# ScalarE's front end steps placed by each sorting stage's share of VectorE's work

## What is computed

```python
corr = jnp.einsum('bmf,bnf->bmn', x3, x3) / F      # x3: layer-normed x, 4 x 4096 x 256
s = -jnp.sort(-corr, axis=-1)
pooled = jnp.take(s, ranks, axis=-1)               # 256 ranks of 4096
...
x = x + pooled
t = layernorm(x)                                   # per token
h = (t @ W_gat); attention over edges -> scores; top 2 of 4 experts, softmax -> g
for ei in range(4):
    hh = gelu(t @ W1[ei] + b1[ei])
    out = out + g[..., ei] * (hh @ W2[ei] + b2[ei])
x = x + out
```

## Time and profile before

| | us |
|---|---|
| median of 3 runs (31820.22 to 31832.84) | 31830.1 |
| the profiled execution | 31848.84 |
| its span in the trace | 31846.8 |
| VectorE busy, share of the span | 28882.6 (91%) |
| TensorE busy | 25804.8 (81%) |
| ScalarE busy | 21288.4 (67%) |
| GpSimd busy | 17887.8 (56%) |

### The profile page before, as it was taken

How to read it: one execution, slowest core, us unless ns; L and a number is a source line. 1 busy time by engine, 2 the same in 40 slices (tenths; PEclk the granted TensorE clock), 3 DMA queues, 4 the chain that set the end, 5 groups by cost and what they waited for, 6 DMA issues and landing times. The chain is left out here.

```text
span 31846.8 us, 518866 instructions
## 1 busy us (share of the span) xinstructions
PE 25804.8 (81%) x174835; PEld 11870.4 (37%) x175348; DVE 28882.6 (91%) x31110; ACT 21288.4 (67%) x31407; POOL 17887.8 (56%) x9076
## 2 busy tenths in 40 slices
PE   3888888888888888888888888888888888863374
PEld 3555533333333333333333333333333333323364
DVE  6888859999999999999999999999999999996744
ACT  1777777777777777777777777777777777750010
POOL 0000018888888888888888888888885000004510
PEclk8999999999999999999999999999999999985655
DMA  2000000000000000000000000000000000001103
GB/s 89 2 2 2 2 18 5 7 6 7 8 7 12 6 7 7 7 7 7 8 12 7 7 6 7 7 7 7 13 7 6 6 6 6 6 5 14 12 11 131
DMA packets 651262, 396.25 MB, mean 12 GB/s; under 512 B 424844, under 2 KB 604048, under 8 KB 646160
## 3 DMA queue, kind: packets, MB, share of 16 engines
q1 hardware_dynamic: 337746, 311.41, 3.1%
q0 software_dynamic: 290304, 22.40, 1.1%
q10 hardware_dynamic: 20288, 25.70, 0.2%
HBM read 196.48 MB, written 162.34 MB: 11 GB/s over the span
## 5 line engine op out<-in xcount | busy, mean ns | idle before, releaser
L1495 POOL DMA_INDIRECT sorted_d<-word_s,place_s x8192 | 16895.5, 2062 | 2644.0 <-issue 2475.4
L1393 ACT ACTIVATE z<-psum 128x1024 f32<-128x1024 f32 x14208 | 14111.6, 1027 | 3637.2 <-PE psum L1154 2513.6
L1154 PE MATMUL psum<-z,net 64*64 64x512 f32 x103424 | 13419.6, 612 | 2473.1 <-ACT z L1393 2318.9
L1352 DVE TENSOR_TENSOR arena<-arena 128x1536 f32<-128x1536 f32 (+17 forms) x6016 | 11646.3, 1936 | 865.1 <-ACT arena L1432 374.8
L1353 DVE TENSOR_TENSOR arena<-arena 128x1536 f32<-128x1536 f32 (+17 forms) x6016 | 11640.5, 1935 | 0.0
L1154 PEld LDWEIGHTS psum<-z,net 64*64 64x64 f32 x103424 | 3103.5, 131 | 11626.9 <-issue 11612.6
L1646 POOL DMA_INDIRECT arena<-table_d,arena x752 | 918.3, 1221 | 5133.2 <-issue 4647.1
L1432 ACT ACTIVATE arena<-arena 128x2048 f32<-128x2048 f32 (+15 forms) x5248 | 3150.1, 600 | 436.3 <-DVE arena L1353 435.9
L979 ACT ACTIVATE arena<-cst,arena 128x128 bf16<-128x128 f32 x8320 | 2633.5, 389 | 606.8 <-PE psum L907 509.8
L1489 POOL DMA_DIRECT2D word_s<-words_d x64 | 37.8, 591 | 4799.3 <-issue 4665.7
L1161 PE MATMUL psum<-z,net 64*128 64x512 f32 x8192 | 1913.4, 600 | 201.5 <-ACT z L1393 190.3
(11 more groups left out here) (218 smaller groups left out, 18950.4 us busy)
## 6 DMA issues: line engine op xcount, KB each, us to landing
sorted_d<-word_s,place_s POOLq DMA_INDIRECT x8192
y_d<-ys SPq DMA_DIRECT2D x256, 256.0 KB, 2.1
arena<-y_d SPq DMA_DIRECT2D x64, 1024.0 KB, 5.6
arena<-in_x SPq DMA_DIRECT2D x34, 512.0 KB, 5.2
x<-in_x SPq DMA_DIRECT2D x65, 256.0 KB, 2.8
xnt_d<-arena SPq DMA_DIRECT2D x32, 512.0 KB, 3.1
hk_d<-arena SPq DMA_DIRECT2D x32, 512.0 KB, 4.3
arena<-hk_d SPq DMA_DIRECT2D x4, 4096.0 KB
```

The source lines that it names most:

```text
L1154: last = nc.tensor.matmul(psum[n * HALF:(n + 1) * HALF, 2 * s + r, :], b.net[rr, at:at + HALF], flat[rr, n * BANK:(n + 1) * BANK], start=T ...
L1352: nc.vector.tensor_tensor(hi_out, hi_in, lo_in, ALU.max)
L1393: last = nc.scalar.activation(flat, bank, ACT.Abs)
L1495: pool.indirect_dma_start(out=b.sorted_d[:, :], out_offset=bass.IndirectOffsetOnAxis(ap=place_s[:, s, j:j + 1], axis=0), in_=word_s[:, s, ...
```

## The change

The ticks are given to halves of stages instead of stages, and not evenly. `half_of` estimates how many elements VectorE handles in a half of stage s, `cost_of` how long a tick takes by its kind, by the FFN pieces behind it and by ScalarE's copies. `spread_ticks` lays the 120 ticks in order over the 96 halves of 48 stages, so that the sums of both run alike; a tick goes behind the carry of the half in which its middle falls. `period` reads the table. The numbers of ticks per half were 1 or 2; now they are 0 to 3. A stage whose half is short (the second of each merge, where the carry is longest) gets fewer ticks, those behind it more.

```diff
--- before.py
+++ after.py
@@ -1064,10 +1064,46 @@
     FRONT_STEPS = N_STAGES - 2
     FRESH_READ = FIRST_MERGE + 1 if LO > 0 else 1
 
-    def ticks_of(step):
-
-        at = [min(PER_PAIR * n // FRONT_STEPS, PER_PAIR) for n in (step, step + 1)]
-        return list(range(*at))
+    ALONE = 150
+    TENSOR = {"corr": 3300, "wires": 2100, "tile": 600, "swapped": 1050, "full": 1050}
+    SCALAR, PIECE, NEWTON = 1080, 1300, 1500
+
+    def half_of(s):
+
+        p, k = STAGES[s]
+        if s >= N_FULL:
+            return sum(2 * op[4] * op[5] * (2 if k > 1 else 1) + ALONE for kind in
+                       (RANK_OPS if k == 1 else SPARSE_OPS[k]) for op in kind) // 2
+        there = M - (LO if s < FIRST_MERGE else 0)
+        later = (3 * P + D if s == ADD_AT else D + NEWTON if s == NORM_AT else 0)
+        return there - (there // p * k if k < p else 0) + 2 * ALONE + later
+
+    def cost_of(tick):
+
+        j, t = TICK_OF[tick]
+        n = SLOTS
+        ats = [tick - EXPERT_TICK - e * EXPERT_TICKS for e in range(EXPERTS)]
+        ups = sum(1 for at in ats if 0 <= at < HC // 2)
+        downs = sum(1 for at in ats if DOWN_AFTER <= at < DOWN_AFTER + 2)
+        return max(n * TENSOR[FRONT[j][t][0]] + 2 * PIECE * (ups + downs), n * SCALAR)
+
+    def spread_ticks():
+
+
+        spans = [half_of(s) for s in range(FRONT_STEPS) for _ in range(2)]
+        costs = [cost_of(tick) for tick in range(PER_PAIR)]
+        scale = sum(spans) / sum(costs)
+        out, at, done, tick = [], 0, 0.0, 0
+        for span in spans:
+            at, here = at + span, []
+            while tick < PER_PAIR and done + scale * costs[tick] / 2 <= at:
+                here.append(tick)
+                done, tick = done + scale * costs[tick], tick + 1
+            out.append(here)
+        out[-1] += range(tick, PER_PAIR)
+        return out + [[] for _ in range(2 * (N_STAGES - FRONT_STEPS))]
+
+    TICKS_BEHIND = spread_ticks()
 
     with nc.Block() as block:
         @block.sync
@@ -1447,12 +1483,10 @@
 
             def period(i, has_next, has_last):
                 for s, (p, k) in enumerate(STAGES):
-                    ticks = ticks_of(s)
                     for g in range(2):
                         if k < p and s < N_FULL:
                             carry(i, s, g)
-                        middle = len(ticks) // 2
-                        for tick in (ticks[middle:] if g else ticks[:middle]):
+                        for tick in TICKS_BEHIND[2 * s + g]:
                             if has_next:
                                 front(i + 1, tick)
                             if has_last:
```

## The result

The changed kernel takes 32187.1 us in the median of four runs (32145.7 to 32218.1), the kernel before beside it 31827.0 (31820.2 to 31832.8). The ratio is **1.0112, 95% interval 1.0099 to 1.0124**. The forecast was +195 us; the measured difference is +360 us. The profiled execution took 32194.5 us, its span is 32192.4. In the rows of after, VectorE's merging stage is L1388 and L1389, its last four stages are L1352, and a product of TensorE is L1190 (L1154 before).

What follows compares the result with a forecast made beforehand. The chain of TensorE's products and ScalarE's copies was taken as the bound, 375.9 us a pair; terms summing to +4.3 made 380.2, +3.15 against 377.05, times 62 pairs +195 us: 32025 us, range 31900 to 32095.

Steps and rivals of the forecast that it cites:

- the front end: Chain of TensorE's products and ScalarE's copies from tick to tick; claimed 375.9 us a pair if never held up.
- Rival 1: Sorting pairs: VectorE is the bound and its waits for carries go, 370.2 us less, so 31460 us; chance 5%.
- (a): Ticks 69 to 75: carries of stages 28 and 29 now stand before ticks 69 to 71; +2.1 us a pair.
- (d): Ticks 25 and 26: the carries of stage 10 move to ticks 24 and 25; -0.8 us a pair.
- (b): Ticks 95 to 102: tick 95 gets GELUs, a 1.91 us carry and copies one after the other; +1.9 us.
- (c): Layer norm's square root and table load move from ahead of tick 20 to plain tick 17; +1.0 us.
- (e): Ticks 1 to 6: carries from before ticks 2 and 3 both stand before tick 1; +0.4 us.
- the base: Front end's length before the change: 377.05 less waits of 0.8 and 0.3, so 375.9 us a pair.
- the low end: All 1.9 us of ScalarE's waits for VectorE delay the front end: length 375.15 us, result 31976 us.
- the high end: The front end's 1.1 us a pair isn't regained: +4.3 x 62 gives 32097 us.

Runs made afterwards that it cites:

- the fillers: Changed kernel with extra TensorE matmuls, whose result nobody reads, ahead of ticks 2, 71 and 96; 31977.5 us, ratio 1.0042.
- the old start: Changed kernel with the even split back in stages 0 to 7; profiled execution, the fastest of four, 32452 us.
- experiment 4: Changed kernel with the even split back in stages 0 to 7, plus two more ticks ahead of the carries of stage 16; 32036.1 us, ratio 1.0056.
- the tight order: Kernel before, with each carry put where TensorE's product is long and not late for VectorE; 31596.7 us, ratio 0.9922.
- The four moves: Kernel before, with carries of stages 9 to 14 later and some of 29, 30, 39, 40 one tick earlier; 31551.1 us (0.9906), second chip 31941.9 (0.9907).
- The half-sort kernels: Kernel before and changed kernel, each with VectorE's minimum left out of the sorting pairs; 39956 and 40331 us, later pairs 374.9 and 382.4 us.

## Why the prediction was right or wrong

**Right: what bounds the kernel.** The step on which the sign rested, that the front end is the nearer chain and that VectorE's waits hide little, held: the front end's own 374.9 us a pair stands above VectorE's 371.1, and with the new order the pair is the front end's length to 0.3 us. Rival 1 (VectorE's gaps as the gain) had no part in it: VectorE's waits before stages 17, 31 and 41 went, and it waits elsewhere, for longer: 2.1 us before stage 19, 2.0 before 29 and 0.9 before 2, as forecast, and 1.3 before stage 10, which I had not named.

**Right: the order's terms.** With the fillers, (a) to (d) came to +1.9, +2.0, +1.0 and -1.1 for +2.1, +1.9, +1.0 and -0.8, and (e) to +0.6 for +0.4. The single ticks named came out too: 70 at 4.57 (4.6), 95 at 5.08 (5.0), 17 at 3.34 (3.2).

**Short in size: the base.** "I take 0.3 as its mean" and 0.8 for the wait at stage 45 gave a hold-up of 1.1 us a pair; with VectorE's minimum left out, the front end is 2.1 shorter. The two waits themselves were sized right (0.84 and 0.27). The other 1.0 us stands at ticks for which the sum had nothing (0, 12, 24, 117, 118), with its cause open. The bound I kept for the low end (375.15 us) came nearer to the length, but for another reason than the one given; its sum is also 3 us off (2.4 x 62 gives 31979, not 31976). The short base makes the result lower, by some 60 us, and hides a part of the other error.

**Wrong, and the one that put the time outside of the range: the durations of TensorE's work were taken as constant.** The sum priced what ScalarE does ahead of a tick and kept all products at the length they had in the trace of before, where the clock is at its upper level almost throughout (1.00 in the earlier trace rows). Two carries, or GELUs and a carry, ahead of one tick make TensorE wait longer at one go than anywhere at those ticks of the kernel before; behind such a wait its clock was often lower, and product and pieces took nearly twice as long, on the chain that sets the pair. That is 382.7 - 379.1 = 3.6 us a pair, 224 us; in the whole run the fillers gave some 225 back, of which up to 73 were already lost in the kernel before. The trace of before did have the sign: 170.7 us at the lower level, with 18 falls in tick 0 alone, behind waits of about 2 us. Neither end of the range held a term for it: the high end, 32095, was the whole order price without any relief, and nothing else. Ticks 71 and 97, which I had put at 3.47 each, are at 4.27 and 4.35; with fillers both are at 3.49. Tick 2, which had no number of its own, is at 3.65 and with fillers at 2.56.

The forecast of VectorE's waits, "9 us a pair in sum", was short for the same reason: 382.7 - 371.1 = 11.6 us (the 815 / 62 = 13 of the rows have in them some of its branch, which stood under <-issue before). That the sort begins 2 to 3 us behind tick 119's copy was wrong in size too: it is 0.37 us; I take it that VectorE's branch is done by the time the copy ends.

## What to carry to other kernels

When an order lets one engine stand longer at one go, price the clock behind that stand too: look in the trace of before for the waits of the length that the change makes, and at the granted clock behind them. Before moving work to take away the waits of the busiest engine, measure the other chain with that engine's work cut. Here the two chains were 1% apart (371.1 and 374.9 us): regions priced one by one missed, and the moves that served both chains gave 0.9%. And see who lives on the waits that are to go: here it was GpSimd's scatter.

## What the runs showed of the hardware

**GpSimd's indirect DMA and VectorE.** In the kernel before, in the two with the old start (experiments 3 and 4) and in the tight order, a scatter was caught in stage 9 of VectorE's sort in 45 to 53 of the pairs. It stood to a later boundary between two of VectorE's instructions, and ended 0.8 to 1.0 us behind it: at VectorE's next wait in the two kernels with the old start (155.14 us to stage 29, 62.22 to stage 17), at boundaries with little or no wait in others (53.43 us to stage 16, 94.13 to stage 21). In the changed kernel none was caught there. With half of VectorE's work cut, the mean of a scatter fell to 1.11 us from 2.06 and none stood over 18 us. So the stand is tied to VectorE's work, and experiment 4 showed that a wait of 1.85 us ends it; the 53 and the 94 us show that less can, too. The four moves left VectorE 86 us of waits for carries and yet had a mean of 1.88 us, so few waits alone don't make it. The Trainium skill (GPSIMD Engine Reference, 1. Specifications) says that GpSimd shares its SBUF interfaces with VectorE and contends with instructions that have two SBUF inputs, as the merging stages have. The rows are in line with it but don't show that this is the reason; they add that a single scatter can stand for 155 us, over many of VectorE's instructions. Why most scatters in the same stretch pass in 1 to 2 us, and a few don't, I can't say. In the kernel before the last scatter ended at 24413 us, which is four fifths of the way through the loop over pairs, not two thirds.

**The same program on another chip.** The kernel before took 32243 us on the second chip and 31846 on the first. The kernel with four moves shows where: its pairs took 380.3 us on the mean from sort 2 to 48, while the scatter ran, and 372.1 from 50 to 62, behind it. In the first stretch ScalarE stood for reasons that aren't in the program, in the rows of the second chip, and not at all on the third; that is 231 us of the some 377 us that the 46 pairs took longer:

```profile
ACT z L1400 <- remote: 231.3, 115, 7.9
```

The cause was not looked for. The half-sort kernels, on the same chip, showed such waits of up to 44 us.
